# Rolling the first groups of an edge stage into loops on VectorE and ScalarE

## The chip, the cores and the metric

The kernel runs on one NeuronCore of a Trainium2 chip. A core has five engines, each with its own stream of instructions: TensorE (PE in the profile; PEld is its weight loads), VectorE (DVE), ScalarE (ACT), GpSimd (POOL) and SyncE (SP, which only starts DMAs here). Each engine has a sequencer that reads its program, waits on semaphores, works on registers and branches; rows with a q behind the engine's name (DVEq, SPq) are work of the sequencer alone. The metric is the time of one execution on the device in microseconds, as the median of several runs.

## The reference

A graph of 6250 nodes (256 features) and 100000 edges, sorted by target node. First a gated edge network, then two hops of a normalised graph convolution with a log-softmax, each with a residual and a layer norm around it:

```
ei   = concat(x[src], edge_attr)                     # 100000 x 320
msg  = sigmoid(ei @ Wg + bg) * (relu(ei @ W1 + b1) @ W2 + b2)
out  = layernorm(segment_sum(msg, dst) + x) * gamma + beta
x    = layernorm(x + out)
h    = two hops of: h = segment_sum(h[row] * norm, col)
x    = layernorm(x + log_softmax(h @ W.T + b))
```

## The kernel before

The edges are cut into 196 groups of 512. The edge stage (about 160 to 1610 us of the run) takes one group after another through a pipeline over all engines:

- SyncE loads the group's edge features `ea`, four groups ahead, in hardware loops (`load_edges`, the loop at L678, the DMA at L661).
- GpSimd gathers 512 rows of a table that already holds `x @ [W1, Wg]` (`gathered`, L797) and works out half of the lower part of the messages.
- ScalarE rounds the edge features (`round_ea`, L1282), copies their transposes out of PSUM (`copy_ea`, L1288), takes the rounded upper part of the hidden rows (`hidden_hi`, L1296) and of the messages (`msg_hi`, L1303), puts the bias under the core products (L1310) and takes the sigmoid (`open_gate`, L1317).
- VectorE works out the lower parts (`ea_split` L1755, `hidden_lo` L1762, `msg_lo` L1787), adds the gate's two terms (L1773), multiplies gate and core product into `room` (L1781), makes the one-hot windows (L1794), and adds the scattered sums of two groups back into `agg` (`add_window`, L1808 to L1813). For that it loads a block number from `base_row` into a register (L1808).
- TensorE does the products: hidden (L946 to L949), gate (L959, L960), core (L972), scatter (L986, L988), and the transposes of the edge features (L935).

Every engine runs a function `step(i, s)` per group, where the group is `2 * i + s`. A step holds pieces of several groups at once: `at_group(stage, i, s, lag)` calls a stage for the group `lag` ahead. The engines are tied to one another only by semaphores that count up; each wait is for a count that follows from the group's number. On VectorE a step's order is: add the window of group g - 2, lower message of g - 1, lower edge features of g + 4, message and one-hot of g, lower hidden rows and gate sum of g + 1. On ScalarE it is: copy the transposes of g + 2, round the features of g + 4, then messages of g between hidden rows of g + 1, bias, sigmoid of g + 1.

Some later groups carry more. On VectorE, from group `begins[0]` = 78 on, each step also has pieces of the node stage (layer norms, degrees), and windows of groups are added in pairs. On ScalarE, from group `begins[1]` = 110 on, rows of the node stage are written too, and at groups 122, 146, 164 and 182 a block of rows for the hops (`upper_rows`).

Before the edge stage the kernel works out whether the edges are in an order that suits it (`fits`). Where they are, as with these inputs, `with act.If(in_order)` and `with dve.If(in_order)` run the fast way. Otherwise a general way runs, whose steps on ScalarE, VectorE and TensorE are already in hardware loops by `over_groups`:

```python
            for g in range(first, 2):
                step(g // 2, g % 2)
            with engine.Fori(1, R - 2) as i:
                for s in range(2):
                    step(i, s)
            for g in range(NG - 4, last):
                step(g // 2, g % 2)
```

In such a loop `i` is a register: waits are for counts worked out from it, and the places of `base_row`, `first_row`, `next_row` and the one-hot's column are addressed by it. In the fast way TensorE, GpSimd, VectorE and ScalarE have all groups written out one behind the other, each wait with its number.

Of the kernel before, what the change touches and what calls it, by code (L numbers as in the profile page):

```python
# [184 lines left out]
def gnn_kernel(nc, x, src, dst, edge_attr, W1, b1, W2, b2, Wg, bg, gamma, beta, Wl, bl, out):  # L185
# [4 lines left out]
    NG = -(-E // GROUP)  # L190
# [18 lines left out]
    DR = DENSE // 2  # L209
    SPARSE = NG - DENSE  # L210
    WIDEST = max(width for _, _, width in RUNS)
    PITCH = plan.span + WIDEST
    assert DENSE % 2 == 0 and (RUN + 1) * P < 2048 and plan.first[0] == 0 and SHARED < plan.first[1]
    assert all((end - first) % many == 0 for first, end, many, _ in plan.runs)
    assert all(w * NB <= 512 or w % 2 == 0 and w * NB <= 1024 for _, _, w in RUNS)
    entry_ends, step_ends = plan.turns(SPARSE)

# [6 lines left out]
    with ExitStack() as ctx:  # L224
# [212 lines left out]
        def at_group(stage, i, s, lag):  # L437

            turn, slot = i + (s + lag) // 2, (s + lag) % 2
            if not isinstance(turn, int) or 0 <= 2 * turn + slot < NG:  # L440
                stage(turn, slot, 2 * turn + slot)
# [36 lines left out]
        begins = [g + 2 for g in complete]  # L478
# [5 lines left out]
        def adds_until(g):  # L484

            if isinstance(g, int) and g > paired.start:
                return g - (min(g, paired.stop) - paired.start + 1) // 2
            return g
# [750 lines left out]
        def _(act):  # L1239
# [93 lines left out]
            def node_rows(c):  # L1333

                first = OWN_ROWS if c == NC - 1 else 0
                for j in range(first, CHUNK):
                    normed_row(c, j)
                for j in range(first, CHUNK):
                    scaled_row(c, j)
# [10 lines left out]
            def step(i, s, in_order=True):  # L1350
                at_group(copy_ea, i, s, 2)
                at_group(round_ea, i, s, 4)
                if in_order and isinstance(i, int):
                    node_rows_at(2 * i + s)
                at_group(upper_msg(0), i, s, 0)
                at_group(upper_hidden(0), i, s, 1)
                at_group(upper_msg(1), i, s, 0)
                at_group(upper_hidden(1), i, s, 1)
                at_group(seed_core, i, s, 1)
                at_group(open_gate, i, s, 1)  # L1360

            def upper_rows(c):

                tiles = slice(CHUNK * c, CHUNK * (c + 1))
                act.wait_ge(S["node_scaled"], rows_until(c))
                if c == NC - 1:
                    act.wait_ge(S["node_work"], NODE_END)
                act.wait_ge(S[f"x3_moved{c}"], 16 * (chunk_copies(c) + KEPT))
                nc.scalar.activation(parts[:, tiles, 0:H], agg[:, tiles, 0:H], ACT.Copy, scale=UPPER).then_inc(
                    S["h0_part_upper"], CHUNK)  # L1370
# [3 lines left out]
            act.wait_ge(S["consts_ready"], 3)  # L1374
            in_order = act.value_load(fits[0:1, 0:1], min_val=0, max_val=1)
            with act.If(in_order):
                for g in range(-4, NG):
                    if g in upper_at:
                        upper_rows(upper_at.index(g))
                    step(g // 2, g % 2)  # L1380
                upper_rows(EARLY)
                for c in range(EARLY + 1, NC):
                    node_rows(c)
                    upper_rows(c)
# [97 lines left out]
        def _(dve):  # L1482
# [275 lines left out]
            def lower_hidden(k):  # L1758

                def stage(turn, s, g):  # L1760
                    dve.wait_ge(S["hidden_upper"], 2 * g + k + 1)
                    nc.vector.scalar_tensor_tensor(out=hidden_lo[:, k, :], in0=banks[:, k, :], scalar=0.0,  # L1762
                                                   in1=hidden_hi[:, k, :].bitcast(F32), op0=ALU.max,
                                                   op1=ALU.subtract).then_inc(S["hidden_ready"], 1)
                return stage
# [160 lines left out]
            def node_stage(c, first, last):  # L1926

                for q in range(first, last):
                    node_piece(c, q).then_inc(S["node_work"], 1)
# [8 lines left out]
            def lower_chunk(k, c):  # L1938
                lower_rows(k, c, slice(CHUNK * c, CHUNK * (c + 1)))

            def node_in_edges(g, place_in):

                for c in range(NC - 1):
                    if begins[c] <= g < begins[c + 1]:
                        if g == begins[c] and place_in == 0:
                            dve.wait_ge(S["agg_added"], adds_until(complete[c]))
                        slots = 6 * (begins[c + 1] - begins[c])
                        slot = 6 * (g - begins[c]) + place_in
                        node_stage(c, NODE_PIECES * slot // slots, NODE_PIECES * (slot + 1) // slots)
                for c in range(EARLY):  # L1950
                    tile = 6 * (g - lower_at[c]) + place_in
                    if 0 <= tile < CHUNK:
                        lower_rows(0, c, slice(CHUNK * c + tile, CHUNK * c + tile + 1))

            def step_in_order(i, s):

                known = isinstance(i, int)

                def node_work_at(place_in):
                    if known:  # L1960
                        node_in_edges(2 * i + s, place_in)

                at_group(add_window, i, s, -2)
                at_group(lower_msg, i, s, -1)
                node_work_at(0)
                at_group(lower_ea, i, s, 4)
                node_work_at(1)
                at_group(message, i, s, 0)
                at_group(one_hot, i, s, 0)
                node_work_at(2)  # L1970
                at_group(lower_hidden(0), i, s, 1)
                at_group(lower_hidden(1), i, s, 1)
                node_work_at(3)
                at_group(add_gate, i, s, 1)
                node_work_at(4)
                node_work_at(5)
# [36 lines left out]
            def square_scales():  # L2013
                dve.wait_ge(S["node_work"], NODE_END)
                nc.vector.tensor_tensor(dinv_square[:, :], dinv[:, :], dinv[:, :], ALU.mult).then_inc(S["dinv_squared"], 1)
# [234 lines left out]
            def wait_scaled():  # L2250
                for c in range(NC):
                    dve.wait_ge(S[f"scaled{c}"], CHUNK)
# [1 line left out]
            so_far = done[0]  # L2254
            in_order = dve.value_load(fits[0:1, 0:1], min_val=0, max_val=1)
            with dve.If(in_order):
                for g in range(-4, NG + 2):
                    step_in_order(g // 2, g % 2)
                dve.wait_ge(S["agg_added"], adds_until(NG))
                lower_chunk(0, EARLY)  # L2260
                node_stage(NC - 1, 0, NODE_PIECES + 2 * OWN_ROWS)
                dve.wait_ge(S["node_work"], NODE_END)
                for c in range(EARLY + 1, NC - 1):
                    lower_chunk(0, c)
                square_scales()
                hop(0)
                wait_scaled()
                hop(1)
# [40 lines left out]
```

## Time and profile before

| | us |
|---|---|
| median of 3 runs (2676.87 to 2678.23) | 2676.89 |
| the profiled execution | 2678.23 |
| its span, first to last instruction | 2676.1 |
| TensorE busy in the span | 2373.5 (89%) |
| VectorE busy | 2079.0 (78%) |
| GpSimd busy | 1662.8 (62%) |
| ScalarE busy | 1493.6 (56%) |

The granted TensorE clock was 0.961 of full speed on the mean. Busy shares are means over stages; the rows further down are from single stretches. Times in the trace count from the span's start. "Idle before, released by" names what ended an engine's idle time; "issue" stands where the trace shows nothing that it waited for. The first number of a row in order of time is the start, the second what it took; neighbouring instructions of an engine overlap by about 0.1 us.

### The profile page before, as it was taken

The page shows a single profiled execution, that of the slowest core. Times are in us where ns is not written, and L with a number is a line of the kernel's source. Part 1 is how long each engine was busy: PE and PEld are TensorE (multiplying, and loading weights), DVE is VectorE, ACT ScalarE, POOL GpSimd, SP SyncE. Part 2 cuts the span into 40 slices and gives each one's busy share as a digit, 9 for nine tenths or more (in the row PEclk, how much of TensorE's full clock was granted, in tenths as well). Part 3 has the DMA queues.
Part 4 walks back from the last instruction along what each step waited for, and adds up shares of the span by engine and source line. Part 5 has one row for each costly group of instructions (what it writes and reads, how often), then busy time and mean ns, then how long its engine had stood idle before and what let it go on. Part 6 is the DMA issues. An engine that isn't in the chain of part 4 may idle for free.

```text
span 2676.1 us, 49629 instructions
## 1 busy us (share of the span) xinstructions
PE 2373.5 (89%) x16049; PEld 1844.8 (69%) x16049; DVE 2079.0 (78%) x4859; ACT 1493.6 (56%) x2727; POOL 1662.8 (62%) x1581
## 2 busy tenths in 40 slices
PE   7889999999999999999999993789888989888874
PEld 3479999999999988988888881344444444444443
DVE  6668888988989888888889998997777763435555
ACT  1157777777777776777767663454666640112123
POOL 0367777777777776766666651456555635666663
PEclk9989999999999999999999996899999999999986
DMA  6555555555555555555555542254455435564542
GB/s 214 202 161 168 171 167 170 168 167 168 173 163 162 164 177 165 159 164 167 167 163 173 158 130 90 81 139 128 120 144 144 132 104 194 197 230 163 188 133 90
DMA packets 276308, 422.59 MB, mean 158 GB/s; under 512 B 127634, under 2 KB 198692, under 8 KB 274004
## 3 DMA queue, kind: packets, MB, share of 16 engines
q0 software_dynamic: 90368, 281.11, 35.5%
q1 hardware_dynamic: 170028, 116.99, 14.8%
q10 hardware_dynamic: 15656, 21.30, 2.3%
q8 instruction: 134, 2.20, 0.3%
q14 instruction: 122, 1.00, 0.1%
HBM read 354.91 MB, written 64.37 MB: 157 GB/s over the span
## 4 chain that ended last, share of the span: by engine, by line
PE 55%; DVE 19%; issue 8%; ACT 7%; another core or an unknown queue 7%; DMA 1%; DVEq 1%; POOL 1%; ACTq 1%; SPq 0%; POOLq 0%
PE banks L972 14%; PE banks L1060 6%; PE banks L949 4%; PE banks L1034 4%; PE banks L1086 3%; PE banks L856 3%; PE banks L1102 3%; PE banks L946 2%; PE banks L947 2%; PE banks L960 2%; PE banks L959 2%; PE banks L988 2%; PE banks L986 2%; DVE codes L1997 2%
## 5 line engine op out<-in xcount | busy, mean ns | idle before, releaser
L797 POOL DMA_INDIRECT gathered<-p_table,src_t x784 | 801.7, 1023 | 413.4 <-DVE gate L1773 225.4
L797 POOL DMA_INDIRECT gathered<-hop_table,src_t x576 | 590.3, 1025 | 444.9 <-PE banks L1102 162.3
L972 PE MATMUL banks<-w_hi,hidden_hi 128*128 128x256 f32 x1568 | 461.4, 294 | 33.4 <-DVE hidden_lo L1762 26.8
L972 PE MATMUL banks<-w_hi,hidden_lo 128*128 128x256 f32 x1568 | 443.9, 283 | 0.0
L972 PE MATMUL banks<-w_lo,hidden_hi 128*128 128x256 f32 x1568 | 443.8, 283 | 0.0
L1427 ACT CAST counts<-banks 128x686 f32 (+3 forms) x382 | 295.7, 774 | 205.1 <-PE banks L1037 85.7
L1303 ACT CAST msg_hi<-room 128x512 fp32r<-128x512 f32 x392 | 242.0, 617 | 228.9 <-DVE room L1781 197.7
L1762 DVE SCALAR_TENSOR_TENSOR hidden_lo<-banks,hidden_hi 128x512 fp32r<-128x512 f32 x392 | 270.3, 690 | 107.6 <-issue 55.1
L1034 PE MATMUL banks<-codes,low_hot 128*128 128x343 f16 (+3 forms) x958 | 243.1, 339 | 103.8 <-DVE codes L1997 55.0
L972 PEld LDWEIGHTS banks<-w_hi,hidden_hi 128*128 128x128 f32 x1568 | 299.9, 191 | 46.7 <-DVE hidden_lo L1762 36.0
L1317 ACT ACTIVATE gate<-gate 128x512 f32<-128x512 f32 x392 | 241.6, 634 | 117.3 <-DVE gate L1773 115.0
L972 PEld LDWEIGHTS banks<-w_lo,hidden_hi 128*128 128x128 f32 x1568 | 300.7, 192 | 0.0
L972 PEld LDWEIGHTS banks<-w_hi,hidden_lo 128*128 128x128 f32 x1568 | 300.3, 192 | 0.0
L1060 PE MATMUL banks<-parts,counts 128*128 128x512 f16 x980 | 287.1, 380 | 0.0
L1296 ACT ACTIVATE hidden_hi<-banks 128x512 fp32r<-128x512 f32 x392 | 234.2, 597 | 51.0 <-PE banks L949 28.4
L1781 DVE TENSOR_TENSOR room<-banks,gate 128x512 f32<-128x512 f32 x392 | 254.0, 682 | 0.8 <-PE banks L972 0.3
L1773 DVE TENSOR_TENSOR gate<-banks,gathered 128x512 f32<-128x512 f32 x392 | 250.8, 680 | 2.9 <-PE banks L960 2.5
L818 POOL TENSOR_TENSOR msg_lo<-room,msg_hi 128x512 fp32r<-128x512 f32 x196 | 237.7, 1213 | 14.0 <-ACT msg_hi L1303 10.0
L1102 PE MATMUL banks<-gathered,hot_half 128*128 128x256 f16 x1152 | 221.9, 283 | 25.3 <-DMA gathered<-hop_table,src_t 14.9
L949 PE MATMUL banks<-ident,gathered 128*128 128x128 f32 x1568 | 236.7, 274 | 0.0
L949 PEld LDWEIGHTS banks<-ident,gathered 128*128 128x128 f32 x1568 | 197.7, 141 | 52.4 <-issue 1.0
L1034 PEld LDWEIGHTS banks<-codes,low_hot 128*128 128x128 f16 x958 | 78.7, 98 | 220.2 <-DVE codes L1997 80.0
(224 smaller groups left out, 5281.0 us busy)
## 6 DMA issues: line engine op xcount, KB each, us to landing
ea<-in_edge_attr SPq DMA_DIRECT2D x196, 128.0 KB
counts_saved<-counts SPq DMA_DIRECT2D x16, 1568.0 KB
ring<-counts_saved SPq DMA_DIRECT2D x16, 1568.0 KB
gathered<-p_table,src_t POOLq DMA_INDIRECT x784
p_table<-p_t ACTq DMA_DIRECT2D x48, 256.0 KB, 3.4
hop_table<-parts SPq DMA_DIRECT2D x12, 896.0 KB
gathered<-hop_table,src_t POOLq DMA_INDIRECT x576
x_saved<-x_room SPq DMA_DIRECT2D x7, 896.0 KB
```

The lines of the kernel that those rows point to most:

```text
L797: pool.indirect_dma_start(out=rows[:, n % slots, j, :], out_offset=None, in_=table[:, :], in_offset=bass.IndirectOffsetOnAxis(ap=src_t[:, ...
L949: last = nc.tensor.matmul(banks[:, k, j * P:(j + 1) * P], gathered[:, s, j, columns], ident[:, :], start=False, stop=j == TILES - 1, is_tr ...
L972: last = nc.tensor.matmul(banks[:, 4 + half, j % 2 * H:(j % 2 + 1) * H], lhs, rhs, start=False, stop=n == len(products) - 1, skip_group_ch ...
L1034: last = nc.tensor.matmul(banks[:, bank, 0:each], low[:, :], code[:, each * n:each * (n + 1)], start=opens, stop=closes and (n > 0 or not ...
L1060: last = nc.tensor.matmul(banks[:, 4 + m % 2, 0:H2], counts[:, b, P * (m % BLOCKS):P * (m % BLOCKS + 1)], parts[:, b, :], start=b == 0, st ...
L1102: last = nc.tensor.matmul(banks[:, bank_of_turn(k, turn), 0:H], hot_half[:, turn % HOT_TURNS * TILES + j, :], hop_rows[:, turn % HOP_SLOTS ...
L1303: nc.scalar.copy(msg_of(msg_hi, s, half), msg_of(msg, s, half)).then_inc(S["msg_upper"], 1)
L1317: nc.scalar.activation(rows, rows, ACT.Sigmoid).then_inc(S["gate_ready"], 1)
L1427: nc.scalar.copy(in_blocks_of(e, coming.pop(0) + shared, width - shared), product_of(e, int(shared))).then_inc(S["evac_done"], 1)
L1762: nc.vector.scalar_tensor_tensor(out=hidden_lo[:, k, :], in0=banks[:, k, :], scalar=0.0, in1=hidden_hi[:, k, :].bitcast(F32), op0=ALU.max, ...
L1773: nc.vector.tensor_tensor(gate[:, tiles, :], banks[:, 2 + half, :].rearrange("p (j n) -> p j n", j=2), gathered[:, s, tiles, H:H2], ALU.ad ...
L1781: nc.vector.tensor_tensor(msg_of(msg, s, half), banks[:, 4 + half, :].rearrange("p (j n) -> p j n", j=2), gate[:, 2 * half:2 * half + 2, : ...
```

## The change

On ScalarE the groups 2 to 109, and on VectorE the groups 2 to 77, are no longer written out. A hardware loop runs over pairs of them; its body is two steps. The groups ahead of them and behind them stay written out. TensorE, GpSimd and SyncE stay as they are.

```diff
@@ scalar: with act.If(in_order)
-                for g in range(-4, NG):
+                for g in range(-4, 2):
+                    step(g // 2, g % 2)
+                with act.Fori(1, begins[1] // 2) as i:
+                    for s in range(2):
+                        step(i, s)
+                for g in range(begins[1], NG):
                     if g in upper_at:
                         upper_rows(upper_at.index(g))
                     step(g // 2, g % 2)
@@ vector: with dve.If(in_order)
-                for g in range(-4, NG + 2):
+                for g in range(-4, 2):
+                    step_in_order(g // 2, g % 2)
+                with dve.Fori(1, begins[0] // 2) as i:
+                    for odd in range(2):
+                        step_in_order(i, odd)
+                for g in range(begins[0], NG + 2):
                     step_in_order(g // 2, g % 2)
```

`begins[0] // 2` is 39 and `begins[1] // 2` is 55, so the loops run 38 and 54 times.

## Rows read from the trace of the kernel before

**Rows 1.** Stretch, length, busy us of PE, PEld, DVE, ACT, POOL; PEclk, DMA, GB/s.

```profile
161.00:700.00 539.00, 536.62 (x4278) 515.48 (x4277) 477.66 (x839) 402.23 (x767) 400.64 (x383) 1.00 0.58 169
700.00:950.00 250.00, 245.42 (x1943) 234.51 (x1942) 222.49 (x422) 180.93 (x350) 183.88 (x174) 1.00 0.56 164
```

**Rows 2.** Order of time on TensorE: start, us, instruction; core products' first.

```profile
503.61 0.36 PE L972 MATMUL banks<-w_hi,hidden_hi 128*128 128x256 f32 x1
...
510.62 0.36 PE L972 MATMUL banks<-w_hi,hidden_hi 128*128 128x256 f32 x1
```

**Rows 3.** Order of time on VectorE, one group, idle time before in brackets.

```profile
502.34 0.69 DVE L1762 SCALAR_TENSOR_TENSOR hidden_lo<-banks,hidden_hi 128x512 fp32r<-128x512 f32 x1 [0.31 <-ACT hidden_hi L1296]
502.95 1.28 DVE L1773 TENSOR_TENSOR gate<-banks,gathered 128x512 f32<-128x512 f32 x2
504.15 0.48 DVE L1813 SCALAR_TENSOR_TENSOR agg<-banks,first_row,agg 128x257 f32 x1
...
504.93 0.68 DVE L1787 TENSOR_TENSOR msg_lo<-room,msg_hi 128x512 fp32r<-128x512 f32 x1
505.71 0.43 DVE L1755 TENSOR_TENSOR ea_split<-ea,ea_split 128x256 fp32r<-128x256 f32 x1
506.05 1.40 DVE L1781 TENSOR_TENSOR room<-banks,gate 128x512 f32<-128x512 f32 x2
```

**Rows 4.** Order of time on ScalarE, from 503 to 515 us.

```profile
503.67 1.23 ACT L1317 ACTIVATE gate<-gate 128x512 f32<-128x512 f32 x2 [0.35 <-DVE gate L1773]
504.80 0.57 ACT L1288 CAST ea_turned_sb<-banks 128x512 fp32r<-128x512 f32 x1
...
508.11 0.60 ACT L1296 ACTIVATE hidden_hi<-banks 128x512 fp32r<-128x512 f32 x1 [0.71 <-PE banks L949]
...
514.73 0.60 ACT L1296 ACTIVATE hidden_hi<-banks 128x512 fp32r<-128x512 f32 x1
```

**Rows 5.** Groups of VectorE, 200 to 700 us: busy, mean; idle before.

```profile
L1762 DVE SCALAR_TENSOR_TENSOR hidden_lo<-banks,hidden_hi 128x512 fp32r<-128x512 f32 x142 | 98.3, 692 | 47.6 <-issue 28.7 <-ACT hidden_hi L1296 18.6
```

**Rows 6.** SyncE's loop records, ns min/median/max: one pass, then 35 passes.

```profile
L678 SPq ALU_OP  x1: 37/37/37, 407.5 to 407.5; - x1
L678 SPq COMPARE_BRANCH  x1: 45/45/45, 407.6 to 407.6; - x1
L678 SPq FUSED_REGOPS  x1: 304/304/304, 407.7 to 407.7; - x1
...
L678 SPq FUSED_REGOPS  x35: 50/303/331, 211.2 to 690.5; - x35
```

**Rows 7.** VectorE's sequencer around the group of rows 3, by line.

```profile
L1808 DVEq TENSOR_LOAD <-base_row x1: 300/300/300, 502.9 to 502.9; - x1
...
L1813 DVEq FUSED_REGOPS  x2: 65/67/69, 503.6 to 503.8; - x2
...
L1780 DVEq EVENT_SEMAPHORE  x2: 21/36/50, 505.7 to 505.9; - x2
```

**Rows 8.** DMA queues that fetch the program: packets, MB, share.

```profile
q8 instruction: 134, 2.20, 0.3%
q14 instruction: 122, 1.00, 0.1%
```

**Rows 9.** Branches at ends of written-out parts: TensorE's, VectorE's, ScalarE's.

```profile
L1227 PEldq COMPARE_BRANCH  x4: 72/198/3772, 1612.9 to 2644.1; - x4
...
2646.51 0.48 DVE L2044 SCALAR_TENSOR_TENSOR agg<-banks,next_of_hop,agg 128x256 f32 x1
2649.38 0.17 DVE L2099 TENSOR_TENSOR last_less<-less_top,lse 128x7 f32<-128x7 f32 x1 [2.39 <-issue]
...
1637.52 1.70 ACT L1369 ACTIVATE parts<-agg 128x1792 f16<-128x1792 f32 x1 [2.74 <-DMA x_saved<-x_room]
1644.40 0.20 ACT L1418 CAST strips<-banks 128x49 f16<-128x49 f32 x1 [5.18 <-issue]
```

## The prediction

> **What bounds the kernel now.** I read the busy shares by stage first. In the stretch that holds groups 2 to 77, TensorE is busy 536.62 of 539 us at full clock, VectorE 478 and ScalarE 402; in the next 250 us, which hold groups 78 to about 110, TensorE is busy 245.42 [rows 1]. So in the whole stretch that the change touches, TensorE stands idle for only 2.38 + 4.58 = 7.0 us. It is the bound there, and neither of the two engines whose code changes is.
>
> Then I read two neighbouring groups in order of time, to see how far behind TensorE the other two are. TensorE starts the core products of one group at 503.61 and of the next at 510.62: 7.01 us a group [rows 2]. On ScalarE and VectorE there is a ring of work that closes once a group: `hidden_hi` (ScalarE), `hidden_lo`, gate sum (VectorE), sigmoid, `ea_turned_sb`, `ea_split` (ScalarE), `ea_split`'s lower part and `room` (VectorE), `msg_hi` and the next `hidden_hi` (ScalarE). From `hidden_hi` at 508.11 to the next at 514.73 nothing in the ring shows an idle time released by TensorE, and it took 6.62 us; the 508.11 itself had waited 0.71 us for TensorE [rows 3, 4]. So the ring has about 7.01 - 6.62 = 0.39 us to spare per group, 0.78 us in the two groups that one loop iteration holds. VectorE's own idle time says the same: 47.6 us in front of 142 `hidden_lo`, 71 groups, is 0.67 us a group [rows 5].
>
> This is the number that the change has to stay under: per iteration of two groups, at most about 0.78 us of new delay in the ring, or TensorE starts to wait.
>
> **The change part by part.** *What is computed.* Nothing is removed: the same VectorE and ScalarE instructions run in the same order with the same waits. VectorE's groups 2 to 77 become 38 iterations of two steps, ScalarE's groups 2 to 109 become 54. The pieces that depend on the group's number (node work, paired windows, upper and lower rows) begin at 78 or later on VectorE and at 110 or later on ScalarE, so no step in the loops had any. TensorE and GpSimd stay written out. That alone costs or gives nothing.
>
> *The back edge.* SyncE already runs such a loop, so its rows price one: the count goes up at 407.5, the branch is taken at 407.6 (0.037 and 0.045 us), and a register record of 0.304 us ends at about 408.05; that last one is between 0.05 and 0.33 us over 35 passes [rows 6]. So a back edge takes the sequencer 0.30 to 0.55 us. On VectorE it falls between the second gate sum and the load of `base_row`, whose place now also comes from a register: one more register record like those of `add_window`, 0.067 us, and its gap, some 0.1 us. Before, the load begins at 502.9 and the second register record ends at 503.87, while the engine is busy with the gate sums until `agg` starts at 504.15 [rows 3, 7]: 0.28 us of cover. With one further register record for the column of `first_row` and the counts waited for (0.1 us), the sequencer needs 0.5 to 0.75 us more, and `agg` starts 0.2 to 0.5 us late. Behind it in VectorE's order are `msg_lo`, `ea_split` and `room`. `ea_split` starts as soon as `msg_lo` is done (504.93 + 0.68 against 505.71), so `room` is late by nearly all of it, and for `room` ScalarE waits.
>
> *The back edge on ScalarE* falls between the second sigmoid and the copy into `ea_turned_sb`. The pair of sigmoids holds the engine from 503.67 to 504.90, and the copy starts at 504.80 [rows 4]; the sequencer is free about 0.5 us before that, since the second sigmoid starts about 504.26 and only short waits stand between. 0.30 to 0.55 us and the registers of two waits leave the copy late by 0 to 0.3 us. It meets VectorE's delay at `ea_split`, where the later one counts, not the sum.
>
> *Waits against registers.* Each wait's count is now worked out from the loop's. Most of that is done while the engine runs an instruction of 0.6 to 0.7 us. One place has little cover: `room` has two waits of its own in front of it (0.050 and 0.021 us), in the 0.34 us between the start of `ea_split` and that of `room` [rows 3, 7]. One or two register records of 0.067 us with their gaps, 0.1 to 0.2 us per step, come through there; 0.2 to 0.4 us per iteration.
>
> *The sum for VectorE's loop.* 0.2 to 0.5 and 0.2 to 0.4 make 0.4 to 0.9 us per iteration, against 0.78 us to spare. I take the middle, 0.65: hidden. The upper end would show 0.12 us in 38 iterations, 4.6 us. Groups differ by some tenths from one another, so I take 1 us. If the cover were gone altogether, 38 x 0.9 = 34 us would be paid.
>
> *The sum for groups 78 to 109.* Here only ScalarE loops, 16 iterations, and VectorE has the node work besides. TensorE's 4.58 us of idle time [rows 1] say that the ring already reaches it now and then. ScalarE's 0 to 0.3 us cost 0 to 4.8 us; I take 2.
>
> *Fetching the program.* The written-out steps come in as 122 packets of 1.00 MB on one queue and 134 of 2.20 MB on the other, 0.1% and 0.3% of the DMA engines' time [rows 8]. The loops save part of the 0.1%: nothing on the path. The other side of it is the branch back. No row shows a branch back over a loop as long as these (some 20 VectorE instructions and waits a group, twice, and registers). SyncE's is short. The nearest rows are forward branches at the end of a written-out part. TensorE's four on one line took 0.072 to 3.772 us, and VectorE, which finished `agg` at 2646.99, started its next instruction at 2649.38 after 2.39 us in which the trace shows nothing that it waited for; ScalarE, between 1639.22 and 1644.40, was idle for 5.18 us, in which a base was loaded besides [rows 9]. So a branch whose target is at hand costs 0.1 to 0.3 us, and one whose target isn't 2.4 to 3.8, with 5.2 as the far end. For 38 iterations I take the first, as SyncE's 35 back edges all show it; the second is a rival below.
>
> The Trainium skill has a rule for this (Runtime: NRT & Kernel Launch, section on instruction fetch mechanics): the sequencer holds two pages of the program and reads ahead only in order, so a taken branch to a page outside them stalls for a fetch, and written-out code is preferred for it. The trace agrees in part: 2.20 MB in 134 packets is that page's 16 KB, but 1.00 MB in 122 is 8 KB, half of it. By that rule a loop that lies across an edge between two pages would miss on every pass, and one that lies inside a page never.
>
> *In all:* +1 and +2 are +3 us. The profiled execution took 2678.23 us (its span of 2676.1 and 2.1 around it), and with the change 2681.2; that execution was 1.3 us above the median of the runs, 2676.89, so against the median I say 2680. A change under 0.2%, 5.4 us, can't be told from none here.
>
> **The rivals.** *The registers come through (slower).* If the loops' overhead in the ring is twice what I worked out, 1.3 us for 0.65, then 0.52 us of each iteration is beyond the 0.78, 38 times: +20 us, and ScalarE's 4.8 us: about 2702. At the upper end (two times 0.9) it is 38 x 1.02 + 4.8 = +44, 2721. For it: TensorE has only 0.39 us a group to give, and a register record can take 0.30 us [rows 6] or 0.067 [rows 7]. Against it: nearly all of them lie under instructions of 0.6 us and more. It decides from 0.92 us per iteration on (0.78 and 5.4 / 38).
>
> *Each back edge misses (slower).* The 2.4 to 3.8 us of [rows 9], less what the second gate sum and the spare time of the ring cover (0.68 and 0.78 us), plus 0.4 us of the ordinary delay, is 1.3 to 2.7 us per iteration: 38 times, +51 to +104 us, middle +77, 2754 (the far end of 5.2 would give +157). ScalarE's further 16 would add 21 to 43 where its loop misses too. For it: the rule above, and the loop's length, perhaps 60 of the 128 instructions of an 8 KB packet if one takes 64 bytes (the page's 16 KB for 256), so about even that an edge falls into it. Against it: nothing shows that the part just left is gone at once, and no back edge of SyncE did it.
>
> *The written-out code was costing something (faster).* If fetching it held up VectorE or ScalarE, the loops give that back. The ceiling is TensorE's idle time in the stretch, 7.0 us of 2677: 2670. Faster by over 0.2% needs 5.4 of these 7.0.
>
> **How the numbers follow.** Hidden, within 0.2%: 0.52, and it is my forecast. Registers come through: 0.26, of which 0.02 stay within 0.2%. Every pass misses: 0.16. Faster: 0.06. That gives faster 0.06, same 0.54, slower 0.40. The range takes in the forecast and the registers' case up to two thirds of its way (2715) and leaves out the misses and half of the faster case: 2673 to 2715.
>
> **What would show each step.** In the profile after: TensorE's 7.01 us from core products to core products should stand unchanged, and its busy time in the first 700 us too. The first `agg` of every second group should start later after the gate sums, by 0.2 to 0.5 us, and the idle time in front of `hidden_lo` shrink from 0.67 us a group to about 0.35. Branch records should show on VectorE's and ScalarE's queues, 37 and 53 of them taken, each below 0.1 us. An idle time of 2 us and more in every second group right after the second gate sum, and more packets on the queue with 122, would show the misses; idle time of TensorE in front of L972, released by `hidden_lo`, the registers. Nothing after 950 us should change by more than it is late.

## The result, and the profile after

The changed kernel takes 2694.11 us, the median of 6 runs (2689.13 to 2702.75). The kernel before took 2678.15 us on the same chip (6 runs, 2676.87 to 2681.54). The ratio is 1.006, 95% interval 1.0044 to 1.0077: 0.6% or 16 us slower. Two executions at a lower granted clock are left out here and below: one of the changed kernel, of 3936 us at 0.555, and one of `e10_scalar_again`, of 3054 us at 0.727.

The changed kernel was profiled twice. The first profile has a span of 2722.1 us, more than any timed run beside it, so it isn't compared as a whole. The second (`e6_after_again` below) is of an execution of 2701.55 us, where the median was 2700.42 and that of the kernel before 2682.66. The stretch in question takes nearly the same time in both (558.8 and 556.8 us, in the table further down). First the second profile's busy times by stretch, columns as in [rows 1]:

```profile
161.00:700.00 539.00, 524.92 (x4122) 497.72 (x4120) 458.81 (x809) 386.34 (x739) 390.19 (x370) 1.00 0.55 162
700.00:950.00 250.00, 243.76 (x1923) 232.08 (x1922) 218.08 (x414) 178.22 (x343) 180.02 (x172) 1.00 0.55 163
```

TensorE now stands idle for 14 us of the first stretch instead of 2.4 [rows 1] (4.5 in `e5_before_again`, the second profile of the kernel before), at the same full clock. Who makes it wait stands in the table of waits from 200 to 700 us (total us, times, longest), same profile:

```profile
ACT hidden_hi L1296 <- PE banks L949: 21.5, 43, 1.2
...
DVE agg L1818 <- issue: 13.1, 23, 0.6
PE banks L972 <- DVE hidden_lo L1767: 10.3, 21, 1.1
ACT hidden_hi L1296 <- remote: 6.6, 7, 1.1
```

The same table of the kernel before (first profile):

```profile
ACT hidden_hi L1296 <- PE banks L949: 12.4, 21, 1.3
...
ACT hidden_hi L1296 <- remote: 2.0, 2, 1.7
...
PE banks L972 <- DVE hidden_lo L1762: 1.8, 2, 1.1
```

The core products wait for `hidden_lo` 21 times; in the kernel before they did so twice, for 1.8 us in all (5 times and 3.7 us in `e5_before_again`). `agg` starts late with nothing that it waited for, at most 0.6 us. And `hidden_hi`, of whose idle time the prediction looked at a single one, waits for TensorE's hidden product for 21.5 + 6.6 = 28 us. In the kernel before it was 12.4 + 2.0 = 14 us already.

One such group in order of time, with the one after the branch: TensorE's first core product of three groups and its last hidden product, then VectorE and ScalarE between them. It answers to [rows 2 to 4].

```profile
501.71 0.39 PE L972 MATMUL banks<-w_hi,hidden_hi 128*128 128x256 f32 x1 [0.28 <-DVE hidden_lo L1767]
...
508.74 0.36 PE L972 MATMUL banks<-w_hi,hidden_hi 128*128 128x256 f32 x1
...
513.05 0.60 PE L949 MATMUL banks<-ident,gathered 128*128 128x128 f32 x4
...
516.22 0.39 PE L972 MATMUL banks<-w_hi,hidden_hi 128*128 128x256 f32 x1 [0.23 <-DVE hidden_lo L1767]
```

```profile
508.15 1.41 DVE L1778 TENSOR_TENSOR gate<-banks,gathered 128x512 f32<-128x512 f32 x2
510.19 0.49 DVE L1818 SCALAR_TENSOR_TENSOR agg<-banks,first_row,agg 128x257 f32 x1 [0.62 <-issue]
...
511.58 0.42 DVE L1760 TENSOR_TENSOR ea_split<-ea,ea_split 128x256 fp32r<-128x256 f32 x1
511.92 1.28 DVE L1786 TENSOR_TENSOR room<-banks,gate 128x512 f32<-128x512 f32 x2
...
515.47 0.69 DVE L1767 SCALAR_TENSOR_TENSOR hidden_lo<-banks,hidden_hi 128x512 fp32r<-128x512 f32 x1 [0.74 <-issue]
```

```profile
508.87 1.36 ACT L1317 ACTIVATE gate<-gate 128x512 f32<-128x512 f32 x2 [0.35 <-DVE gate L1778]
510.14 0.57 ACT L1288 CAST ea_turned_sb<-banks 128x512 fp32r<-128x512 f32 x1
...
513.40 0.60 ACT L1296 ACTIVATE hidden_hi<-banks 128x512 fp32r<-128x512 f32 x1
513.90 0.62 ACT L1303 CAST msg_hi<-room 128x512 fp32r<-128x512 f32 x1
514.84 0.60 ACT L1296 ACTIVATE hidden_hi<-banks 128x512 fp32r<-128x512 f32 x1 [0.33 <-PE banks L949]
```

One group takes 7.03 us, the next 7.48. In the longer one `agg` is 0.62 us late, and with it `room` and `msg_hi`. The first `hidden_hi` starts at 513.40, when TensorE's count for it comes (513.38 in the trace; ScalarE was free at 513.26). The second `hidden_hi` is later still: it waits 0.33 us more for TensorE and starts at 514.84, 6.10 us after the core products at 508.74. From there on nothing has slack: `hidden_hi` 0.60, `hidden_lo` at 515.47 with 0.69, core products at 516.22, 1.38 us later.

The two back edges in the first profile of the changed kernel (count, ns min/median/max, first and last start): VectorE's and ScalarE's over the whole loops, then VectorE's at one iteration with the load behind it. They answer to [rows 6, 7].

```profile
L2264 DVEq FUSED_REGOPS  x38: 74/74/74, 172.2 to 716.9; - x38
L2264 DVEq ALU_OP  x38: 40/40/40, 187.6 to 730.9; - x38
L2264 DVEq COMPARE_BRANCH  x38: 50/56/67, 187.7 to 730.9; - x38
...
L1379 ACTq FUSED_REGOPS  x54: 59/59/65, 172.9 to 952.6; - x54
L1379 ACTq ALU_OP  x54: 35/35/35, 188.3 to 968.2; - x54
L1379 ACTq COMPARE_BRANCH  x54: 40/45/50, 188.4 to 968.3; - x54
...
L2264 DVEq ALU_OP  x1: 40/40/40, 481.2 to 481.2; - x1
L2264 DVEq COMPARE_BRANCH  x1: 56/56/56, 481.3 to 481.3; - x1
L2264 DVEq FUSED_REGOPS  x1: 74/74/74, 481.4 to 481.4; - x1
...
L1813 DVEq TENSOR_LOAD <-base_row x1: 303/303/303, 481.6 to 481.6; - x1
```

And VectorE itself in order of time at that iteration, same profile:

```profile
480.36 1.50 DVE L1778 TENSOR_TENSOR gate<-banks,gathered 128x512 f32<-128x512 f32 x2
482.48 0.49 DVE L1818 SCALAR_TENSOR_TENSOR agg<-banks,first_row,agg 128x257 f32 x1 [0.62 <-issue]
```

No branch took more than 0.067 us. From the count at 481.2 to the load at 481.6 it is 0.37 us (481.185 and 481.556 in the trace), from the load to `agg` 0.93. The two gate sums end at 481.86, so `agg` is 0.62 us late. And the queues that fetch the program, in the page of the same profile, against [rows 8]:

```profile
q8 instruction: 136, 2.23, 0.3%
q14 instruction: 101, 0.83, 0.1%
```

### The profile page after: what moved, and what is told of

Same layout as the page of the kernel before. It is cut to its first block, busy times and chain, and to the rows that moved or that the text cites. A ratio compares the mean times of both kernels' runs of the same rounds, so it can differ in the third digit from the quotient of the medians.

```text
span 2722.1 us, 50965 instructions
## 1 busy us (share of the span) xinstructions
PE 2389.6 (88%) x16049; PEld 1845.0 (68%) x16049; DVE 2076.2 (76%) x4860; ACT 1493.1 (55%) x2727; POOL 1663.0 (61%) x1581
## 4 chain that ended last, share of the span: by engine, by line
PE 53%; DVE 18%; issue 9%; ACT 8%; another core or an unknown queue 7%; DMA 2%; DVEq 1%; POOL 1%; ACTq 1%; SPq 0%; POOLq 0%
PE banks L972 15%; PE banks L1060 5%; PE banks L949 5%; PE banks L1034 4%; PE banks L1086 3%; PE banks L856 3%; ACT counts L1432 2%; PE banks L1102 2%; PE banks L946 2%; DVE hidden_lo L1767 2%; PE banks L947 2%; ACT hidden_hi L1296 2%; DVE room L1786 2%; PE banks L960 2%
## 5 line engine op out<-in xcount | busy, mean ns | idle before, releaser
L972 PE MATMUL banks<-w_hi,hidden_hi 128*128 128x256 f32 x1568 | 462.1, 295 | 55.1 <-DVE hidden_lo L1767 48.6
L972 PE MATMUL banks<-w_lo,hidden_hi 128*128 128x256 f32 x1568 | 443.6, 283 | 0.0
L972 PE MATMUL banks<-w_hi,hidden_lo 128*128 128x256 f32 x1568 | 443.5, 283 | 0.0
L972 PEld LDWEIGHTS banks<-w_hi,hidden_hi 128*128 128x128 f32 x1568 | 299.6, 191 | 79.0 <-DVE hidden_lo L1767 66.5
L972 PEld LDWEIGHTS banks<-w_lo,hidden_hi 128*128 128x128 f32 x1568 | 300.3, 191 | 0.0
L972 PEld LDWEIGHTS banks<-w_hi,hidden_lo 128*128 128x128 f32 x1568 | 300.0, 191 | 0.0
```

The costliest lines, as they stand in the source:

```text
L972: last = nc.tensor.matmul(banks[:, 4 + half, j % 2 * H:(j % 2 + 1) * H], lhs, rhs, start=False, stop=n == len(products) - 1, skip_group_ch ...
```

## The experiments

Twelve kernels were run in three series of four; the kernels of a series ran on one chip, between runs of the kernel before. The kernel before itself took 2729.15 us in the first series (24 runs), 2682.66 in the second (29) and 2724.83 in the third (21); the second and the third were on the same chip. So each kernel is set against before of its own series, and the traces are used to compare across them. The kernel before was profiled in the second series only.

**Series 1: one loop at a time.** `e1_vector_only` is the change on VectorE alone, `e2_scalar_only` on ScalarE alone (the two hunks of the diff above). `e3_vector_four` has the body of VectorE's loop twice as long, `e4_vector_turned` the same body begun at another place, so that the branch falls between `one_hot` and `hidden_lo`, where VectorE has idle time:

```diff
 e3: four groups a pass
+                with dve.Fori(0, (begins[0] - 2) // 4) as j:
+                    for turn in range(2):
+                        for odd in range(2):
+                            step_in_order(2 * j + 1 + turn, odd)
 e4: first = add_window .. one_hot, last = lower_hidden .. add_gate
+                step_in_order(1, 0, last=False)
+                with dve.Fori(1, begins[0] // 2 - 1) as i:
+                    step_in_order(i, 0, first=False)
+                    step_in_order(i, 1)
+                    step_in_order(i + 1, 0, last=False)
+                step_in_order(begins[0] // 2 - 1, 0, first=False)
+                step_in_order(begins[0] // 2 - 1, 1)
```

> Only VectorE's groups 2 to 77 are looped, ScalarE is written out as before. Theory A (VectorE's back edge and register work make its part of the ring late): nearly all of the 16 us of the change, +12 to +16 us against before. Theory B (ScalarE's back edge, 54 times, in front of its copy): 0 to +4 us. Theory C (the two delays only matter together, since the ring passes both engines): well under 12, about +5 us.

> Only ScalarE's groups 2 to 109 are looped, VectorE is written out as before. Theory A: 0 to +4 us. Theory B: +12 to +16 us. Theory C: about +5 us, so that this and the run with VectorE's loop alone add up to clearly less than 16.

> VectorE's loop alone with a body of four groups: 19 passes and half the back edges, the same waits against registers. If the back edge is what costs: half of the run with VectorE's loop alone, +6 to +8 us where that is +12 to +16. If the waits and addresses worked out from registers are what costs (theory D): the same as that run.

> VectorE's loop alone, with the body turned: the branch falls between the one-hot and hidden_lo, where the engine was idle for 0.3 to 0.7 us in every group of before, and not ahead of the window's addition. 37 passes. Theory A with the place of the back edge as the cause: 0 to +4 us. Theory D (registers, wherever the branch is): as much as the run with VectorE's loop alone.

Measured against before (2729.15): e1 2710.23, ratio 0.9933 (0.9909 to 0.9958); e2 2748.9, 1.0078 (1.0051 to 1.0105); e3 2710.84, 0.993 (0.9913 to 0.9948); e4 2717.25, 0.9967 (0.9947 to 0.9988). None of the theories, as they stand above, had VectorE's loop faster than the written-out code and ScalarE's alone slower by 20 us at once. Half as many back edges (e3) gave nothing over e1, and another place for the branch (e4) nothing either. So on VectorE the price of the back edge isn't what decides, and theories A, B and C fail. D had e3 and e4 cost as much as e1, but none of them costs anything.

What does decide is seen in e2's trace, and again in its repeat e10, the profile shown here: one of its long groups, on TensorE and on ScalarE.

```profile
478.24 0.36 PE L972 MATMUL banks<-w_hi,hidden_hi 128*128 128x256 f32 x1
...
482.55 0.60 PE L949 MATMUL banks<-ident,gathered 128*128 128x128 f32 x4
...
486.53 0.39 PE L972 MATMUL banks<-w_hi,hidden_hi 128*128 128x256 f32 x1 [1.05 <-DVE hidden_lo L1767]
```

```profile
482.29 0.59 ACT L1296 ACTIVATE hidden_hi<-banks 128x512 fp32r<-128x512 f32 x1
482.79 0.61 ACT L1303 CAST msg_hi<-room 128x512 fp32r<-128x512 f32 x1
485.15 0.60 ACT L1296 ACTIVATE hidden_hi<-banks 128x512 fp32r<-128x512 f32 x1 [1.76 <-remote]
```

The records have TensorE's second hidden product done at 483.15. ScalarE, free at 483.40, starts its `hidden_hi` at 485.15, when TensorE's semaphore count comes. The kernel before needs some 0.2 us for this step. It isn't this count alone: those of the two gate products and of the scatter come in one burst behind it, at 485.19, 485.25 and 485.34 in the trace, where their last records end at 483.62, 484.10 and 485.05; the count of the transposes comes at 485.50, just behind its record (485.49). The gate and scatter matmuls between can't have been done in 0.2 us, so TensorE did its work in time and only its counts were held, about until the scatter was through. Other late groups are alike, as far as the counts have records: 31 such counts in e2 and 35 in e10 come 6.92 us (median) after the core products, the scatter's 0.21 us behind, the transposes' at 7.26 or 7.27, where their records end. The group takes 8.29 us instead of 7.01, and 31 of e2's 38 even groups last 7.9 us or more.

**Series 2: before and after again, an extra load, both branches moved.** By now there were two theories: R, that the registers and branches delay the ring as the prediction's rival said, and P, that the small delays matter through the phase between the engines, on which the late count of TensorE depends. `e5_before_again` (e5) is the kernel before and e6 the changed kernel, both as they are. e7 is the kernel before with one more load:

```diff
                 for g in range(-4, NG + 2):
+                    if 2 <= g < begins[0] and g % 2 == 0:
+                        dve.value_load(base_row[0:1, 0, 0:1], min_val=0, max_val=NB - 1)
                     step_in_order(g // 2, g % 2)
```

e8 is the change with VectorE's loop turned as in e4 and ScalarE's too, its branch behind `round_ea`, where ScalarE waits some 1.1 us for `room`:

```diff
+                step(1, 0, last=False)
+                with act.Fori(1, begins[1] // 2 - 1) as i:
+                    step(i, 0, first=False)
+                    step(i, 1)
+                    step(i + 1, 0, last=False)
+                step(begins[1] // 2 - 1, 0, first=False)
+                step(begins[1] // 2 - 1, 1)
```

> The kernel before, unchanged but for a comment, to have its profile from the same chip as the experiments. Both theories: a ratio of 1.000 within 0.2%. Theory R (registers in the ring): TensorE's core products come every 7.02 us in groups 2 to 77 here too, and hidden_hi on ScalarE hardly ever waits for a signal that is late. Theory P (the second half of the hidden product is signalled late on every other group, and which kernel meets it depends on the phase of the engines): where this kernel takes 2729 us instead of 2678, its groups take 7.3 to 7.6 us, and the idle time of hidden_hi in front of its second half is tens of us in the stretch from 200 to 700 us.

> The changed kernel, unchanged but for a comment. Theory R: 1.006 again (1.004 to 1.008), groups 2 to 77 at 7.3 to 7.4 us. Theory P: the ratio differs from 1.006 by more than the intervals allow, since on a chip where the kernel before takes 2729 us it already pays for late signals: between 0.993 (VectorE's loop alone) and 1.008 (ScalarE's alone), and the group time follows the idle time that hidden_hi has ahead of its second half.

> Everything written out, and VectorE's sequencer given one more register load of base_row ahead of every second group from 2 to 76, 38 of them: about 0.5 us of sequencer work (a load of 0.30 us and what follows it) where the loop's back edge stood. Theory R: this is the loop's cost without a loop; agg starts some 0.5 us late in every second group, and the kernel is slower than before by 8 to 20 us, 1.003 to 1.008. Theory P: it moves VectorE's phase just as the loop did, so it comes out where VectorE's loop alone came out, 0.990 to 0.997.

> Both loops, their bodies turned so that each branch falls where its engine has idle time: VectorE's ahead of hidden_lo, ScalarE's behind round_ea, ahead of the messages. Theory R: nearly all of the back edges' cost is hidden, so it is faster than the change by 6 to 16 us and within 0.2% of the kernel before, or below it. Theory P: the places of the branches matter only through the phase; no better than the change by more than 5 us, and the groups alternate between 7.0 us and longer as before.

Measured against before (2682.66): e5 2682.63, ratio 0.9998 (0.9987 to 1.0009); e6 2700.42, 1.0058 (1.0041 to 1.0075); e7 2689.53, 1.0024 (1.0011 to 1.0037); e8 2689.51, 1.0021 (1.0005 to 1.0036). The change's 0.6% repeats, as R says and P denies, and its groups 2 to 77 take 7.33 us in the mean, as R says too. The extra load costs 7 us, a little under the 8 to 20 of R and outside of P's 0.990 to 0.997. In its waits from 200 to 700 us `agg` is late as R says, but less than by the load's 0.5 us:

```profile
DVE agg L1813 <- issue: 7.6, 25, 0.8
```

That is 0.3 us each time, and the even groups stay at 7.00 us: a delay of `agg` of this size is hidden. The 7 us are only in part in e7's profile: its groups 2 to 77 take 3.5 us more than e5's, in a few single groups, even and odd, and nothing behind them takes longer. With both branches moved 11 of the 18 us come back, as R says and P denies, though e8 is at the edge of R's 0.2% from before. Busy times by stretch of e8:

```profile
161.00:700.00 539.00, 536.98 (x4239) 512.20 (x4238) 473.00 (x831) 396.29 (x760) 394.51 (x379) 1.00 0.57 167
```

TensorE is as busy in the first stretch as it was before the change [rows 1], so what e8 still costs in its timed runs isn't in this profile, whose own time was 2686.69. So P as it was put on record failed with e6, e7 and e8, and R narrowly with e7; e5 couldn't tell them apart.

**Series 3: each loop again, each branch moved alone.** e9 repeats e1, e10 repeats e2. e11 is the change with only ScalarE's branch moved, e12 with only VectorE's (diffs as above).

> VectorE's loop alone, a second time, for another chip. Theory V (VectorE's back edge ahead of agg is what is paid): +8 to +16 us against the kernel before, as the whole change, and core products 7.5 to 7.7 us apart in every second group. Theory S (ScalarE's loop is what is paid): within 3 us of before. Theory J (each loop's delay fits into the some 0.6 us by which hidden_lo is ahead of TensorE, both together do not): 0 to +4 us, nearly every group at 7.0 to 7.1.

> ScalarE's loop alone, a second time. Theory V: within 3 us of before. Theory S: +8 to +16 us, and on a chip where the kernel before takes about 2680 us every second group of 2 to 77 at 7.5 us or more, as in its first run (8.3). Theory J: 0 to +4 us.

> The change with ScalarE's branch moved behind round_ea, where ScalarE waits for room anyway; VectorE's loop as in the change. Theory V: no better than the change, +13 to +17 us against before. Theory S: within 3 us of before. Theory J: half of the loss back, +4 to +10 us, like both loops turned (+7).

> The change with VectorE's branch moved ahead of hidden_lo, where VectorE has idle time; ScalarE's loop as in the change. Theory V: like both loops turned, +4 to +9 us against before. Theory S: no better than the change, +13 to +17. Theory J: half of the loss back, +4 to +10.

Measured against before (2724.83): e9 2708.93, ratio 0.9944 (0.9923 to 0.9966); e10 2746.57, 1.0089 (1.0057 to 1.0121); e11 2723.42, 0.9996 (0.9978 to 1.0015); e12 2754.03, 1.0111 (1.008 to 1.0141). By the ratios theory S comes nearest, that ScalarE's loop is what is paid, but of its figures only e11's held (e9 is 16 us faster than before and e10 and e12 22 and 29 us slower); V and J fail. The traces say that this isn't the whole of it. The table is worked out from each trace: the time from the first core product of group 2 to that of group 78; the median length of the groups with an even number (the branches of unturned loops fall into them) and with an odd one; and the median time from an even group's first core product to the second `hidden_hi` in it.

| kernel | series | groups 2 to 77, us | even | odd | second `hidden_hi` |
|---|---|---|---|---|---|
| before (the first profile) | | 535.4 | 7.00 | 7.02 | 5.11 |
| before, e5 | 2 | 538.6 | 7.00 | 7.02 | 5.11 |
| changed (the first profile) | | 558.8 | 7.69 | 7.05 | 6.30 |
| changed, e6 | 2 | 556.8 | 7.52 | 7.04 | 6.12 |
| extra load, e7 | 2 | 542.1 | 7.00 | 7.02 | 5.22 |
| both turned, e8 | 2 | 540.2 | 7.09 | 7.05 | 5.70 |
| VectorE's loop, e1 | 1 | 539.2 | 7.04 | 7.05 | 5.63 |
| VectorE's loop, e9 | 3 | 544.9 | 7.08 | 7.04 | 5.70 |
| VectorE's, four groups, e3 | 1 | 541.4 | 7.03 | 7.02 | 5.48 |
| VectorE's, turned, e4 | 1 | 548.5 | 7.03 | 7.04 | 5.53 |
| ScalarE's loop, e2 | 1 | 578.4 | 8.30 | 7.04 | 6.93 |
| ScalarE's loop, e10 | 3 | 580.6 | 8.30 | 7.05 | 6.93 |
| both, ScalarE's turned, e11 | 3 | 557.4 | 7.69 | 7.05 | 6.31 |
| both, VectorE's turned, e12 | 3 | 581.8 | 8.37 | 7.04 | 6.99 |

Three things are to be read in it.

First, in all fourteen traces a group in which the second `hidden_hi` starts later than 5.7 us after the core products lasts 1.38 us longer than that, in the median: 6.12 and 7.52, 6.93 and 8.30. It can start as late as 7.01 - 1.38 = 5.63 without cost. That is the whole length of the long groups.

What makes it late can be worked out from the same traces. From the first `msg_hi` to the second `hidden_hi`, with a `hidden_hi` and a `msg_hi` between, it is 1.52 or 1.53 us where ScalarE has no idle time in it (median, in each of the twelve traces that aren't of the kernel before). So a first `msg_hi` up to 5.63 - 1.52 = 4.11 us after the core products costs nothing. That `msg_hi` waits for `room` alone, so its start carries all that VectorE and ScalarE are late by up to there. In the even groups it starts at 3.48 us in e5, 3.98 in e1, 3.88 in e6 and 3.53 in e2 (medians), and in e6 and e2 never later than 4.01 and 3.68. So without the two `hidden_hi`'s waits for TensorE's counts no even group of e6 or e2 would have been longer.

Second, the effects don't add. VectorE's loop alone leaves the groups at 7.0 to 7.1; ScalarE's alone makes every second one 8.3; together they come to 7.5 to 7.7, less than ScalarE's alone. Moving one branch of the two leaves the stretch as it was (e11) or makes it longer (e12). Only with both moved is the stretch back at 540, 16.6 of the 18.2 us between e6 and e5. So e11's ratio of 1 is no sign that the move helped: its stretch is as long as the change's. The first profile of the changed kernel, with its span of 2722.1 us, is as long as the kernel before is in that series.

Third, the stretch of one and the same kernel hardly depends on the series (e6 and the first profile of the change, e1 and e9, e2 and e10). What lies behind it does: from the core products of group 195 to the end e5 to e8 take 1077 to 1080 us, the kernels of series 1 and 3 1084 to 1098, and the groups 78 to 194 take 891 to 895 us against 897 to 911.

## Why the prediction was right in part and wrong in its likeliest case

The time fell into the range, 2673 to 2715, but not where the forecast had it: 16 us slower instead of 3. The rival "The registers come through" had the size (+20) and the place (idle time of TensorE ahead of L972, released by `hidden_lo`), but not the mechanism. So it is luck that the range holds: it was made wide for another cause, and no term of the prediction stands for the one that the runs show.

- **TensorE bounds the stretch at 7.01 us a group: right.** The whole loss is in groups 2 to 77, 18.2 us between e6 and e5; the groups 78 to 194 took 3.5 us less and the rest 1.0 us more.
- **The back edge on VectorE, `agg` 0.2 to 0.5 us late: right for VectorE's loop alone.** There it is 0.29 late (median of the even groups in e1 and in e9). In the changed kernel it is 0.62. The back edge takes 0.37 us, as worked out (0.30 to 0.55). The cover is smaller. In the kernel before the load begins at 502.9, as the first gate sum does, with both of them, 1.3 us, to hide it [rows 3, 7]. In the changed kernel's even group the second gate sum itself waits for TensorE (the pair takes 1.50 us for 1.28), the sequencer gets past it only at 481.19, and has one gate sum of 0.69 us for 1.3 us of work.
- **The registers of `room`, 0.2 to 0.4 per iteration: wrong.** From `ea_split` to `room` it is 511.58 to 511.92, 0.34 us, as in [rows 3]. Nothing comes through.
- **ScalarE's copy 0 to 0.3 late: right, and beside the point.** The copy starts at 510.14, before the second sigmoid's record ends (510.23), as in [rows 4].
- **0.78 us to spare per iteration: wrong, and it is the first step that failed, though the 16 us don't come from it.** The spare time of two groups was added up. But ScalarE and VectorE meet TensorE again in every group, so a delay in the even group has only that group's spare to go into: for the first `msg_hi` from 3.48 to 4.11, 0.63 us. VectorE's loop alone moves it to 3.98 and 3.97 (e1, e9) and so uses 0.5 of it. The forecast for this part, hidden, held: the stretch is 0.6 and 6.3 us longer than e5's, which was measured in another series.
- **The ring closes without TensorE: wrong, and it is where the 16 us are.** The prediction counted the ring as work of ScalarE and VectorE alone, and put TensorE's part in it at nothing. It goes through TensorE's hidden product, whose counts come late when the loops run. In e6's even groups the delay of VectorE and ScalarE alone would have the second `hidden_hi` at 4.01 + 1.52 = 5.53 at the latest, and up to 5.63 is free; it starts at 6.12. In the mean the even groups take 0.58 us more than in e5 and the odd ones 0.10 less: 0.48 us in each of 38 iterations are 18 us. e2 and e10 show it without VectorE's loop, and larger (6.93). A sign of it stood in the trace before: 23 waits of `hidden_hi` for TensorE, 14 us in 500, and the 0.71 us of [rows 4] are one of them, for a product whose record ends at 507.62 and whose count comes at 508.02.
- **Groups 78 to 109, +2 us: wrong in size.** 232.6 us in e6, 233.0 in e5.
- **Each back edge misses: refuted** by the records of 0.040 to 0.067 us for all 38 and 54 branches, and by the fetch queue: 101 packets instead of 122. The prediction weighed the rule of the Trainium skill (Runtime: NRT & Kernel Launch, on instruction fetch mechanics) that a branch to a page outside the two held stalls; these loops show no such stall on any pass, which goes with the rule only if both lie inside what is held. The prediction took it that a loop across an edge between two pages would miss on every pass; the rule itself speaks of a window of two pages, and a pass here has 58 records on VectorE (110 in e3, whose branches take 0.056 us too) and 38 on ScalarE.
- **The written-out code costs something: not so in the series of the result.** The changed kernel, e6 and e8 are all slower than the written-out code there. In the other two series VectorE's loop alone is 16 to 19 us faster than before, more than the ceiling of 7.0 us, and why is not known.

What stays open is why TensorE's counts come late, and why the loops make it more frequent. The dependence on small delays (in e10's even groups `agg` starts 1.05 us after the core products for 0.86 in e5, and `room` 2.82 for 2.76, in the median) and the sums that don't add would go with the phase between engines: each late group would put the ring back to where it started, and two groups later it would be late again. That is argued and not shown, and theory P, the same thought, failed in its figures. Neither a particular transfer nor an access to a bank was shown to hold it. It also stays open why VectorE's loop alone is 0.6% faster than before where before takes 2725 to 2729 us. Taking the parts outside the stretch from e1's and e9's traces leaves the stretch of before 16 to 22 us more there than it has in e5, as 12 to 17 late counts of 1.3 us would; but before was not profiled in those series, so this was only argued. No kernel here beats before in the series where it takes 2683; VectorE's loop alone was not run there.

## What to carry to other kernels

Spare time can't be pooled over iterations when the late engine meets the bounding one once in each: work out for each step of the body the latest start that costs nothing (here 5.63 us after the core products for the second `hidden_hi`), and compare the delay with that. Before a ring of work is priced without the bounding engine, add up every wait that a finished instruction of that engine is said to have ended (here 14 us in the trace before), and look whether its count came late. In a kernel whose ring is 0.4 us shorter than its bound, effects needn't add: against e5 the stretch takes 1 and 6 us more with VectorE's loop alone, 40 and 42 with ScalarE's alone (both in other series) and 18 with both, so each combination has to be run. And compare only with the kernel before in the same series, since it alone moved by 1.6% on one chip.

## What was not expected of the hardware

- A taken branch back over two groups' instructions (58 records on VectorE, 38 on ScalarE) is cheap: 0.040 + 0.056 + 0.074 us of records on VectorE, 0.035 + 0.045 + 0.059 on ScalarE, on every pass, though the program is fetched from memory.
- TensorE's completion count can come 2.0 us behind the modelled end of the matmul that gives it (483.15 and 485.13 in e10), at the full granted clock and with the matmul records at their regular places; the counts behind it are held too and come in a burst (four in 0.21 us). An idle time "released by remote" or by a matmul long done is worth looking at, even if it is rare: the kernel before had 2 of the first kind in 500 us, and 21 that name the hidden product's last matmuls.
- The same kernel took 2682.66 us and 2724.83 us on the same chip in two series, and kernels profiled in the slower ones spend 4 to 21 us more in the part behind the last group.
